# Layer norm of batch 1 in the recurrence's tail, attention that begins with batch 1's projections, projections in row halves of TensorE, residual in column halves

## What is computed

```python
x = conv_ref(x, ...)                              # recurrence f + b, group norm, silu, + x
t = to_tokens(x)                                  # (4, 1024, 64)
t = t + attn_ref(ln_t(t), Wq, Wk, Wv)             # softmax(q k^T / 8, causal) v
t = t + ffn_ref(ln_t(t), sigma, phi, M_u, M_phi_plus, M_phi_minus, ...)

def ln_t(v, eps=1e-5):                            # layer norm over the 64 channels of a token
    m = mean(v, -1); s = var(v, -1)
    return (v - m) / sqrt(s + eps)
```

## Time and profile before

| | |
|---|---|
| median of 3 runs | 915.15 us (912.4 to 916.39) |
| the profiled execution | 911.7 us, its span 909.9 us |
| busy over the span | PE 90%, DVE 74%, ACT 65%, POOL 59% |
| attention begins, slot 0's fourth block is done, experts begin | 464.4, 498.1, 611.9 us |

### The profile page before, as it was taken

The page is one execution under the profiler, slowest core; times in us unless marked ns, Lnnn a source line. Parts: engine busy times, 40 slices in busy tenths (PEclk is TensorE's granted clock), DMA queues, the critical chain, the costliest instruction groups (busy, mean ns, idle before and its releaser), DMA issues. The chain is left out here.

```text
span 909.9 us, 10954 instructions
## 1 busy us (share of the span) xinstructions
PE 823.3 (90%) x3238; PEld 505.1 (56%) x3238; DVE 677.8 (74%) x742; ACT 591.7 (65%) x941; POOL 536.5 (59%) x367
## 2 busy tenths in 40 slices
PE   5598899979999898977979999989999999999997
PEld 1243443434444343433435555558888888888886
DVE  2889999999989999998953664647666565565665
ACT  3887869788787979876626456556555554555554
POOL 4688989899998998887947952412121221212220
PEclk9699999999999999997987999999999999999999
DMA  6969897788959788694639300003334242243432
GB/s 150 342 225 320 276 303 267 310 294 301 308 200 387 262 299 316 251 331 165 232 44 158 104 1 1 1 1 93 124 107 139 92 139 94 93 139 96 135 107 78
DMA packets 72470, 165.67 MB, mean 182 GB/s; under 512 B 24194, under 2 KB 25236, under 8 KB 72420
## 3 DMA queue, kind: packets, MB, share of 16 engines
q1 hardware_dynamic: 72436, 165.27, 56.1%
HBM read 162.99 MB, written 2.26 MB: 182 GB/s over the span
## 5 line engine op out<-in xcount | busy, mean ns | idle before, releaser
L479 POOL TENSOR_TENSOR prod<-hidden,c_wide 128x1024 f32<-128x1024 f32 x127 | 298.1, 2361 | 43.3 <-DVE hidden L1067 35.8
L591 PE MATMUL ps_y<-prod,ident 128*128 128x512 f32 x508 | 239.6, 612 | 21.7 <-ACT ps_y L766 12.1
L1067 DVE TENSOR_TENSOR_SCAN hidden<-decay,ps_d 128x1024 f32<-128x1024 f32 x97 | 221.3, 2282 | 11.8 <-PE ps_d L582 3.3
L2100 PE MATMUL ps_conv<-hankel,u_high 128*128 128x512 f32 (+1 forms) x768 | 212.5, 358 | 0.1
L591 PEld LDWEIGHTS ps_y<-prod,ident 128*128 128x128 f32 x508 | 94.6, 194 | 141.3 <-issue 121.1
L2100 PEld LDWEIGHTS ps_conv<-hankel,u_high 128*128 128x128 f32 x768 | 138.5, 189 | 24.7 <-DVE u_t L1963 0.3
L2100 PE MATMUL ps_conv<-hankel,u_low 128*128 128x512 f32 (+1 forms) x384 | 137.2, 357 | 0.0
L1928 POOL CAST block_mix<-even 128x256 fp32r (+1 forms) x32 | 12.7, 397 | 204.9 <-PE sums L1969 204.9
L2217 DVE TENSOR_TENSOR stack<-ps_conv,stack 64x512 fp32r<-64x512 f32 x128 | 88.3, 690 | 60.2 <-ACT stack L2184 57.7
L2217 DVE TENSOR_TENSOR qk<-ps_conv,qk 64x512 fp32r<-64x512 f32 x128 | 88.2, 689 | 48.3 <-ACT qk L2184 45.7
L2184 ACT ACTIVATE stack<-ps_conv 64x512 fp32r<-64x512 f32 x128 | 76.0, 594 | 72.5 <-PE ps_conv L2100 70.6
(11 more groups left out here) (298 smaller groups left out, 1192.3 us busy)
## 6 DMA issues: line engine op xcount, KB each, us to landing
c_wide<-bc_rows SPq DMA_DIRECT2D x128, 512.0 KB, 4.7
b_wide<-bc_rows SPq DMA_DIRECT2D x104, 512.0 KB, 5.6
hankel<-filters SPq DMA_DIRECT2D x32, 1026.0 KB, 5.3
plus<-in_M_phi_plus SPq DMA_DIRECT2D x2, 1024.0 KB, 13.0
minus<-in_M_phi_minus SPq DMA_DIRECT2D x2, 1024.0 KB, 17.4
x_pair<-in_x SPq DMA_DIRECT2D x2, 768.0 KB, 9.2
bc_rows<-mixed_and_low SPq DMA_DIRECT2D x8, 128.0 KB, 4.0
out<-plus SPq DMA_DIRECT2D x8, 128.0 KB, 3.5
```

The costliest lines, as they stand in the source:

```text
L479: nc.gpsimd.tensor_tensor(prod[k % PAIR][:, :], hidden[k % DEEP][:, :], c_wide[s % BC_DEEP][:, :], ALU.mult).then_inc(prod_ready, 1)
L591: mm = nc.tensor.matmul(out, ident[:, :], halves(prod[k % PAIR])[h], start=False, stop=True, skip_group_check=True)
L1067: nc.vector.tensor_tensor_scan(hidden[k % DEEP][:, order], left[:, order], right[:, order], 0.0, ALU.mult, ALU.add).then_inc(hidden_ready, 1)
L2100: mm = nc.tensor.matmul(out, pairs[q][wp][:, 2 * delta + source, :], rows, start=(delta == 0 and term == 0), stop=(delta == 2 * half + 1 a ...
```

## The change

It has four parts.

1. **Layer norm of batch 1 moved into the recurrence.** `next_tokens` (8 transposes on PE into `ps_x`) stands ahead of `last_out(0)`; `center_next` and `spread_x(1)` on DVE between `last_product` and `last_gate`; `square(1)` on ACT; `rstd(1)` on POOL; `norm_next`, one DVE instruction in place of ACT's eight, behind `last_gate`. The tokens themselves (`tok`, for the residual) are still made in attention, by `tokens(1)`.
2. **The beginning of attention.** It starts with `normed(1)` and interleaves queries, keys and values of batch 1 with the pieces of batch 0, and then already does blocks 0 to 3 of slot 0. `tokens(2)` moves from n = 3 to n = 4. The group norm of batch 3 moves back: `norm_stats`/`norm_scale` on DVE behind all reductions, `norm_silu` on ACT to n = 6 of slot 0, its residual on POOL behind six matrices. On POOL `rstd(2)` moves forward, to behind three matrices.
3. **Row halves.** `xn_t` holds the first 512 tokens in partitions 0 to 63 and the other 512 in 64 to 127, and the weights are held twice (5 more loads of 16 KB at the program's start). Queries and keys are 4 matmuls of 256 columns (in the recurrence 2 of 512), values 8, in turn from the two halves, each half into its own PSUM bank. ACT's copies of `xn_t` and of the values in the recurrence become two each.
4. **Column halves.** The residual of the second batch of a pair goes to PSUM partitions 64 to 127 and alternates with the first batch's.

```diff
+def project_halves(nc, banks, w, xn_t, step=SPAN):
+    for at in range(0, H, step):
+        for h in range(2):
+            rows = slice(h * C, (h + 1) * C)
+            mm = nc.tensor.matmul(banks[h][:, at:at + step], w[rows, :, :].rearrange("d j e -> d (j e)"),
+                                  xn_t[rows, at:at + step], start=True, stop=True)
+    return mm
+def value_halves(nc, banks, w, xn_t):
+    for t in range(TILES // 2):
+        for h in range(2):
+            rows = slice(h * C, (h + 1) * C)
+            mm = nc.tensor.matmul(banks[h][:, t * C:(t + 1) * C], xn_t[rows, t * 128:(t + 1) * 128], w[rows, :],
+                                  start=True, stop=True)
+    return mm
...
+                def next_tokens():
+                    pe.wait_ge(drive_ready, driven_before(2 * B - 1, N - 1, True) + 1)
+                    turn_x1(1, ps_x)
...
+                def norm_next():
+                    dve.wait_ge(ln_rstd, 2)
+                    nc.vector.tensor_tensor(xn[1][:, :, :], cen[1], a.small[:, 2, :].unsqueeze(2).to_broadcast([128, TILES, C]),
+                                            ALU.mult).then_inc(xn_ready, 1)
...
                 last_product()
+                center_next()
+                spread_x(1)
                 last_gate()
+                norm_next()
...
-                rstd(1)
                 filter_rows(nc, pool, e)
                 norm_rstd(nc, pool, g, a.minus_half, B - 1)
+                weigh_and_sum(nc, pool, e, 0, 3)
+                rstd(2)
+                weigh_and_sum(nc, pool, e, 3, EXPERTS + 2)
                 pool.wait_ge(g.act_ready, B)
                 nc.gpsimd.tensor_tensor(x1[:, (B - 1) * L:], g.mixed[:, :], x1[:, (B - 1) * L:], ALU.add).then_inc(g.x1_ready, 1)
-                weigh_and_sum(nc, pool, e, 0, EXPERTS + 2)
-                rstd(2)
                 weigh_and_sum(nc, pool, e, EXPERTS + 2, 2 * EXPERTS)
...
-                        if after and n == 3:
+                        if after and n == (3 if b else 4):
                             tokens(b + 2)
...
-                tokens(1)
+                normed(1)
                 scores(0, 0, 4)
...
-    for b in range(2):
-        for a in range(2):
-            for delta in range(SPANS):
-                dst = (e.low[0:C, b, a, :], e.mid[0:C, b, a, :], e.tail[b][0:C, a, 0:HEAD],
-                       e.tail[b][0:C, a, HEAD:])[delta]
+    for a in range(2):
+        for delta in range(SPANS):
+            for b in range(2):
+                rows = lanes(b)
+                dst = (e.low[rows, b, a, :], e.mid[rows, b, a, :], e.tail[b][rows, a, 0:HEAD],
+                       e.tail[b][rows, a, HEAD:])[delta]
                 mm = add_out(nc, dst, x2[:, 2 * delta + a, 2 * q + b, :], att.ident[:, :])
```

More of the change, by code:

```diff
@@ L666, in batch, with turn_x1 @@
                                 first_attention[s]()
+                def turn_x1(b, out):
+                    for t in range(TILES):
+                        delta, parity = divmod(t, 2)
+                        mm = nc.tensor.transpose(out[:, t * C:(t + 1) * C],
+                                                 x1[:, b * L + SPAN * delta + parity:b * L + SPAN * (delta + 1):2], ident[0:C, 0:C])
+                    mm.then_inc(tok_psum, 1)
                 def tokens():
@@ L682, in normed @@
                     for t in range(TILES):
-                        mm = nc.tensor.transpose(ps_w[0:C, t * 128:(t + 1) * 128], xn[:, t, :], ident[:, :])
+                        mm = nc.tensor.transpose(ps_w[0:C, t * 128:(t + 1) * 128], xn[0][:, t, :], ident[:, :])
                     mm.then_inc(xnt_psum, 1)
                 def queries_or_keys(w, done):
-                    for h, out in enumerate(halves(ps_w)):
-                        mm = nc.tensor.matmul(out, w[:, :, :].rearrange("d j e -> d (j e)"), xn_t[:, h * H:(h + 1) * H],
-                                              start=True, stop=True)
-                    mm.then_inc(done, 1)
+                    project_halves(nc, halves(ps_w), w, xn_t, step=H).then_inc(done, 1)
                 def queries():
@@ L886, in last_unit @@
                         act.wait_ge(xnt_psum, 1)
-                        nc.scalar.activation(xn_t, ps_w[0:C, :], ACT.Copy).then_inc(xnt_ready, 1)
+                        for h, part in enumerate(halves(ps_w)):
+                            taken = nc.scalar.activation(xn_t[h * C:(h + 1) * C, :], part[0:C, :], ACT.Copy)
+                        taken.then_inc(xnt_ready, 1)
                         shared_decay_of(u, i, LAST_SHARE[2], xnt_ready, 1, True)
@@ L1291, in project @@
                 def project(w, done):
-                    for h in range(2):
-                        mm = nc.tensor.matmul(ps_p[:, h, :], w[:, :, :].rearrange("d j e -> d (j e)"),
-                                              halves(xn_t)[h], start=True, stop=True)
-                    mm.then_inc(done, 1)
+                    project_halves(nc, [ps_p[:, h, :] for h in range(2)], w, xn_t).then_inc(done, 1)
                 def queries(b):
@@ L1382, in turn_back, with slot @@
                     mm.then_inc(back_psum, 1)
-                def slot(b):
+                def slot(b, begun=0):
                     ahead, after = b + 1 < B, b + 2 < B
-                    for n in range(BLOCKS_T):
+                    for n in range(begun, BLOCKS_T):
                         if n + 2 < BLOCKS_T:
@@ L1433, in _ @@
                 scores(0, 6, 8)
-                normed(1)
+                keys(1)
+                scores_t(0, 0)
+                scores_t(0, 1)
                 scores(0, 8, 10)
                 maxima(0, 2, rows=2, back=0)
+                values(1)
+                attend(0, 0)
+                scores_t(0, 2)
                 scores(0, 10, 12)
-                queries(1)
-                scores_t(0, 0)
-                scores_t(0, 1)
-                keys(1)
+                attend(0, 1)
+                scores_t(0, 3)
                 maxima(0, 3, rows=3, back=0)
-                for b in range(B):
+                attend(0, 2)
+                tokens(1)
+                scores_t(0, 4)
+                attend(0, 3)
+                scores_t(0, 5)
+                slot(0, begun=4)
+                for b in range(1, B):
                     slot(b)
@@ L1529, in slot @@
                         take_output(b - 1, 1)
-                    exp(b, 0)
-                    if ahead:
-                        take_k(b + 1)
-                    row(b, SPANS - 1)
-                    for n in range(BLOCKS_T):
+                        exp(b, 0)
+                        if ahead:
+                            take_k(b + 1)
+                        row(b, SPANS - 1)
+                    for n in range(0 if b else 4, BLOCKS_T):
                         if n == 4:
@@ L1686, in slot @@
                     ahead, after = b + 1 < B, b + 2 < B
-                    if ahead:
+                    if ahead and b:
                         split_k(b + 1)
```

170 lines of the change are left out of this document (94 added, 76 removed).

## The result

| | before | after |
|---|---|---|
| median, first group of runs | 915.37 us (912.4 to 917.22, 6 runs) | 905.94 us (904.8 to 908.83, 6 runs), ratio 0.9903, 95% interval 0.9881 to 0.9925 |
| median, second group | 912.97 us (21 runs) | 908.21 us (9 runs), ratio 0.9949, 0.9927 to 0.9971 |
| profiled execution, span | 911.7, 909.9 us | 906.72, 904.9 us |
| start of the last product (DVE) to the end of the span | 453.8 us | 448.1 us; 448.0 in the second group |

The change makes the kernel faster. By how much is less sure than one group suggests: 9.4 us in the first, 4.8 in the second. Most of the spread lies in the recurrence. In 13 profiles of these kernels its last product starts anywhere from 456.1 to 464.1 us, and from there to the end the changed kernel took 448.1 and 448.0 us in its two profiles.

What follows compares the result with a forecast made beforehand. PE, busy for 90% of the span, was taken to bound the kernel, with POOL limiting slot 1. 5.9 (POOL) + 1.7 (row halves) + 1.5 (column halves) - 0.5 (clock) = 8.6 us; 915.15 - 8.6 = 906.5 us, range 901 to 911.

Steps and rivals of the forecast that it cites:

- End of the recurrence: Gate on DVE at the recurrence's end: 0.3 to 1.1 us later, 0.6 taken.
- Beginning of attention: PE up to block 3 of slot 0: done 21.7 us after the start instead of 33.7, 11.4 us gained after the late start.
- the beginning gains little: Rival at attention's start: maxima, queries and exponentials wait on one another; 7.8 us gained in all, 907.3 us; no separate chance.
- Tokens of batch 2 at n = 4: PE at piece 2 of batch 1 in slot 0: a stall of 2.0 us, costing 1.7 us.
- POOL: Slots 0 and 1: POOL's dense row sets the scaling of batch 3 on ACT, so 5.9 us are gained there.
- Row halves: PE's projections: halves overlap, 0.65 us saved each on queries and keys, 0.4 on values; 1.7 us for batch 3.
- Column halves: PE's residuals before the experts: second pair's saves 1.5 us, first pair's nothing.
- 0.5 for a fall of the clock: Term subtracted in the sum: PE's clock falls behind the stalls, costing 0.5 us.
- halves don't overlap: Rival on PE: alternating tiles saves nothing for row or column halves; gain 4.9 us, 910.2 us; chance 0.18.
- column halves do nothing in PE: Rival in PE's residuals: only column halves give nothing; gain 7.1 us, 908.0 us; chance 0.15.
- a change of halves drains PE: Rival on PE: each change costs p, gain 4.9 - 35 p, 917 us at p = 0.19; chance 0.08.
- POOL doesn't hold: Rival in slots 0 and 1: PE's own gain stands instead of POOL's limit; 14.6 us, 900.5 us; chance 0.13.

Runs made afterwards that it cites:

- tokens_3: Changed kernel with batch 2's tokens turned at n = 3 instead of 4 in slot 0: 446.9 us from last product to end, against 448.1; ratio 0.9936.
- before_pool: Kernel before with POOL's power for batch 2 one weighed matrix earlier: 453.6 us from last product to end, against 453.8; ratio 0.9986.
- pool_first: Changed kernel, POOL's power for batch 2 ahead of the first weighing, slot 1's two powers ahead of the even matrices: 439.9 us from last product, ratio 0.985.
- best_tail: Kernel of best with batch 2's tokens as in tokens_3 and batch 3's second-norm scaling on DVE instead of ACT: 437.4 us from last product, ratio 0.9793.
- best: Changed kernel with pool_first's POOL order, batch 3's residual addition one matrix earlier, column halves in second pair alone: 438.8 us from last product, ratio 0.9849.

## Why the prediction came out as it did

The median was forecast at 906.5 and came at 905.94, but 8.6 us of gain were summed up and the stretch from the last product shows 5.7. The profiled execution was to take 903.1 and took 906.72. The median hit by luck: the first group's medians lay 9.4 us apart, those of the second 4.8; the sum was 2.9 us too high. By places, 5.9 us were forecast at the scaling of batch 3 and 2.6 came, 1.7 from there to the experts and 2.3 came, and 1.0 among the experts (1.5 for the residual less 0.5 for the clock) and 0.8 came.

- **End of the recurrence** (0.3 to 1.1 late, 0.6 taken): 0.2. Just under the range, because the values save 0.9 us.
- **Beginning of attention** (block 3 after 21.7 us): 19.5. The mechanism is right; the fall of the clock that was reckoned in didn't come, and block 3 is 14.0 us earlier instead of 11.4. That the beginning gains little is out.
- **Tokens of batch 2 at n = 4** (a stall of 2.0): 1.92. As tokens_3 shows, this stall is mostly hidden behind POOL.
- **POOL.** This step failed. Its first half held: `weigh_and_sum` began at 490.99 (489.3 forecast), `rstd(2)` at 501.81 (500.1), the even matrices ended at 535.36 (533.6), `rstd(3)` at 538.79 (536.9), everything 1 to 1.2 us late by the last product; before_pool shows that POOL's order held at most 0.5 us before, pool_first that its order and its work beside DVE hold 8.2 us now. But "5.9 us are gained, whatever PE saved before" took POOL for the last wait at the scaling of batch 3. ACT came from the row of maxima at 540.52, 1.7 us after POOL. The sum had no price for DVE beside POOL: in slot 1 before the change POOL had finished the even matrices at 528.54 and was idle when DVE's small instructions ran; the change moved both into the same stretch.

  2.6 us came instead of 5.9, and the 3.3 that are missing divide so. 0.5 is a slip in the sum: it took POOL's new end, 536.9, from ACT's old start, 542.80; POOL's old end was 542.27. 1.2 is POOL's own lateness, 1.0 of it the later start of `weigh_and_sum`, which waits for a transfer. The other 1.6 is PE, which makes the row of maxima: DVE's long instructions stall it for 2.20 us, and behind the stall its clock falls, so that the same work takes 4.80 us instead of 3.19 (tokens_3). Where the clock didn't fall, the stall alone put the maxima no further behind POOL than they were before the change, 0.5 us.

  The Trainium skill, "SBUF — State Buffer", SBUF: two separate sides, states this rule: a DVE instruction that runs in a two-port mode, or has two SBUF inputs while the GpSimd instruction reads SBUF, and a GpSimd instruction lock each other out for a whole instruction. The traces agree: L1681 has two SBUF inputs and took 2.44 us beside POOL and 0.69 without, L1663, with one in PSUM, 0.69 in both cases, and the small instruction 1.79 and 0.17. No view shows in which mode the small one ran. I had not asked of the new order which DVE instructions fall beside POOL.
- **Row halves** (1.7 for batch 3): a projection takes 1.06 to the next start, 0.85 saved each (forecast 0.65); the values save 0.9 (forecast 0.4). That is 2.6 us for batch 3's three, and 2.3 came from the scaling of batch 3 to the experts: the mechanism was right, the saving at a change of halves was put too low.
- **Column halves** (1.5 from the second pair, 0 from the first): 3.71 to 1.97, 1.74 in the second pair. The first pair's 0 was right for the residual itself, but wrong for what follows: PE idles for 3.23 us and the clock costs 1.2 to 1.3, so "0.5 for a fall of the clock" was too little.

  The rule of the Trainium skill, "TensorE: Matmul & The Clock Gate", Part 3 (The mechanism), that a weight load overlaps with running matmuls only when its row group differs, is not borne out: here both column halves use the same rows, and 32 passes with their loads took 1.97 us in alternation and 3.33 in turn. The kernel before spoke against it too: PE's passes and weight loads are busy for 823.3 and 505.1 us of a span of 909.9.
- **Rivals.** That halves don't overlap, that column halves do nothing in PE, and that a change of halves drains PE are out by these durations. "POOL doesn't hold" is out for this kernel; moving POOL's powers ahead comes near that case, 5.7 + 8.2 = 13.9 us beside the 14.6 it was priced at.

## What to carry to other kernels

When an engine is freed early, list for the new order which DVE instructions now run beside POOL's long ones. An instruction of 8 elements a partition can take 2 us there (2.15 and 2.30 in `best_tail` and `best`), and if a power on POOL waits for it behind matrices, the waits chain. Put short instructions that others wait for ahead of long ones that nobody waits for yet. Shorten a stretch of PE only where PE ends it: in front of a wait it saves nothing and can cost the clock. Where two profiles of one kernel differ, compare from a landmark just ahead of the change, and look at the granted clock behind each stall before a gain of 1 us is put down to an edit.

## What was unexpected of the hardware

- Two row halves or two column halves of TensorE overlap without strict alternation. At one change of halves some 3 passes are saved (values 2.00 to 1.60 us, residual 3.71 to 3.33); with groups of 4 passes the overlap is nearly full (1.16 against 1.11). Eight passes of 256 columns, four of each half, take 1.07 us to the next start in either order. The single records of the trace fit that: the passes of the values in turn start at 0, 0.16, 0.27, 0.38 and 0.50 us, counted from the first; from there to 0.88 two series of starts run side by side, each 0.11 us apart, and then one again. So the other half's first pass starts beside the fifth of the first half's eight. In the residual in turn it is the thirteenth of sixteen, at 1.37 us. The records don't name the half; that the second series is the other half is my reading.
- The granted clock behind the wait in front of the experts: with 0.30 to 1.79 us of idle time the first transposes took 1.06 or 1.07 us (six profiles), with 2.88 to 3.28 the clock fell to between 0.57 and 0.68 for the 4 us behind (five profiles). Between them it isn't settled by idle time alone: with 2.28 us it fell to 0.66, with 2.45 it stayed at 1.00, and behind the stall of 2.2 us in slot 1 it fell in four profiles and not in three. A fall costs 1.2 to 1.3 us in front of the experts and up to 1.6 in slot 1.
- The recurrence is 8 us shorter or longer from run to run, with a mean clock up to 450 us of 0.95 in `best` (last product at 456.9) and 0.93 in tokens_3 (464.1). The clock isn't all of it: in pool_first it is 0.95 too, with the last product at 462.6. The cause stays open.
